# Second attention: the attended values leave their bank on VectorE, behind the routing steps, and no longer on ScalarE

## The reference

```python
# second attention (H = 8 heads of DH = 128; context and tokens are its keys and values)
xn = _layernorm(x, gamma_media, beta_media); ln = _layernorm(latents, gamma_lat, beta_lat)
q = ln @ Wq + bq
k, v = split(concatenate([xn, ln], axis=1) @ Wkv + bkv)
sim  = einsum('bhid,bhjd->bhij', q * DH ** (-0.5), k)
attn = softmax(sim, axis=-1)
out  = einsum('bhij,bhjd->bhid', attn, v) ... @ Wo + bo
x = x + tanh(g_xattn[1]) * out
# second expert layer: the two best of 8 experts for each token
logits = xf @ router_w.T; top_w, top_i = lax.top_k(softmax(logits), 2)
...
x = x + tanh(g_ffn[1]) * sum over the two of share * w_down(silu(w_gate x) * (w_up x))
```

## Time and profile before

| what | value |
| --- | --- |
| median of 3 timed runs | 1478.63 us (1478.35 to 1478.68) |
| profiled execution, first to last instruction | 1498.2 us |
| PE busy | 1377.6 us, 92% of the span |
| DVE busy | 953.4 us, 64% |
| ACT busy | 1012.3 us, 68% |
| POOL busy | 523.2 us, 35% |
| copy of the attended values (L2051, ACT) | 64 times, 616 ns in the middle |

### The profile page before, as it was taken

How to read it: one execution, slowest core, us unless ns; L and a number is a source line. 1 busy time by engine, 2 the same in 40 slices (tenths; PEclk the granted TensorE clock), 3 DMA queues, 4 the chain that set the end, 5 groups by cost and what they waited for, 6 DMA issues and landing times. The chain is left out here.

```text
span 1498.2 us, 33716 instructions
## 1 busy us (share of the span) xinstructions
PE 1377.6 (92%) x12029; PEld 1171.5 (78%) x12029; DVE 953.4 (64%) x2374; ACT 1012.3 (68%) x2019; POOL 523.2 (35%) x510
## 2 busy tenths in 40 slices
PE   5898699899999999999999999988999999876985
PEld 4887588788888888888888888877778888755773
DVE  6998767666766767667667666552455555654455
ACT  5887487577677676776776767647788888633552
POOL 3112355322322322323223223302235555635553
PEclk9999899999999999999999999999999999998998
DMA  8300100399940000000000000022000000022236
GB/s 221 88 1 1 58 2 1 77 176 102 102 30 2 2 1 2 2 2 2 2 2 1 2 1 2 1 73 57 1 29 14 17 16 16 30 69 63 76 97 174
DMA packets 124980, 60.46 MB, mean 40 GB/s; under 512 B 41945, under 2 KB 120241, under 8 KB 124690
## 3 DMA queue, kind: packets, MB, share of 16 engines
q1 hardware_dynamic: 120274, 48.92, 18.2%
q0 software_dynamic: 4544, 9.38, 1.9%
HBM read 28.84 MB, written 29.44 MB: 39 GB/s over the span
## 5 line engine op out<-in xcount | busy, mean ns | idle before, releaser
L1349 DVE SCALAR_TENSOR_TENSOR hidden<-psU,b_cols,gelu 128x512 f32<-128x512 f32 x256 | 191.4, 750 | 170.1 <-ACT gelu L1474 104.9
L1474 ACT ACTIVATE gelu<-psG,b_cols 128x512 f32<-128x512 f32 x256 | 176.2, 689 | 109.6 <-PE psG L142 96.2
L1296 POOL TENSOR_TENSOR combine_sum<-combine_sum,combineT 128x512 f32<-128x512 f32 x48 | 63.3, 1319 | 294.9 <-ACT combineT L1488 294.9
L1325 POOL TENSOR_TENSOR dispatchT<-dispatchT,dispatch_inv 128x512 f32<-128x512 f32 x64 | 67.7, 1057 | 232.6 <-DVE dispatch_inv L1453 232.6
L1608 PE MATMUL psU<-w_down,hidden 128*64 128x128 f32 x2048 | 123.4, 273 | 0.0
L1608 PE MATMUL psDown<-w_down,hidden 128*64 128x128 f32 x2048 | 122.7, 273 | 0.0
L1861 POOL TENSOR_TENSOR probs<-probs,row_sum 128x512 f32<-128x512 f32 x64 | 66.2, 1035 | 143.6 <-DVE row_sum L1974 142.6
L1608 PEld LDWEIGHTS psU<-w_down,hidden 128*64 128x64 f32 x2048 | 113.2, 137 | 1.3 <-issue 1.2
L1608 PEld LDWEIGHTS psDown<-w_down,hidden 128*64 128x64 f32 x2048 | 113.9, 137 | 0.1
L140 PE MATMUL psG<-slots_hi,w_gate_hi 128*128 128x512 f32 x256 | 105.9, 414 | 1.1 <-ACT gelu L1474 0.6
L2038 ACT ACTIVATE probs<-psS,neg_max 128x128 f32<-128x128 f32 x256 | 91.2, 384 | 22.8 <-DVE neg_max L1971 18.4
(11 more groups left out here) (406 smaller groups left out, 3617.6 us busy)
## 6 DMA issues: line engine op xcount, KB each, us to landing
sorted_x<-empty_rows SPq DMA_DIRECT2D x1, 12736.0 KB, 77.5
tile_rows<-sorted_x SPq DMA_DIRECT2D x78, 65.0 KB
sorted_x<-empty_rows SPq DMA_DIRECT2D x1, 4544.0 KB, 29.9
expert_ys<-expert_y SPq DMA_DIRECT2D x16, 256.0 KB, 3.7
x<-in_x SPq DMA_DIRECT2D x8, 256.0 KB, 5.9
ctx<-in_ctx SPq DMA_DIRECT2D x8, 256.0 KB, 5.9
w_gate_raw<-in_L_ffn_Wg SPq DMA_DIRECT2D x1, 2048.0 KB, 10.9
w_up_raw<-in_L_ffn_Wu SPq DMA_DIRECT2D x1, 2048.0 KB, 16.1
```

What stands on the lines that cost most here:

```text
L1325: pool.tensor_tensor(e[:], e[:], over(rb[:], SEQ, 2), ALU.mult).then_inc(s["eb_normed"], 1)
L1349: dve.scalar_tensor_tensor(hid[e][:, half, :], U[half][:], bcol[:, 1, 4 * ch + 2 * e + half:][:, 0:1], gel[half][:], ALU.add, ALU.mult).th ...
L1474: act.activation(gel[half][:], G[half][:], ACT.Gelu, bias=bcol[:, 0, 4 * ch + 2 * e + half:][:, 0:1]).then_inc(s["gelu"], 1)
```

## The change

The copy from `Y` to `yT` moves from ScalarE to VectorE. On ScalarE it stood behind the copy of the turned probabilities (and a query eviction) of the same slot and ahead of the input evictions and of ScalarE's routing steps. On VectorE it stands at the end of the slot, behind `route(o, j)`. Its two waits move with it: for the value product (`av`), and for the output product that last read this half of the buffer (`out`). The engine operation becomes a tensor copy, with the same source and destination. Nothing else is changed; lines behind the insertion move by seven.

```diff
@@ VectorE, slot()
                 route(o, j)
+                if exists(o, j, 3):
+
+                    m = (j - 3) % OB
+                    need(dve, s["av"], n - 2)
+                    need(dve, s["out"], 4 * o + (j - 3) // 2 - 1)
+                    dve.tensor_copy(yT[(m // 2) % 2][:, :, (m % 2) * SEQ:(m % 2 + 1) * SEQ],
+                                    Y[:].rearrange("p (h n) -> p h n", h=H)).then_inc(s["yT"], 1)
@@ ScalarE, slot()
                 if 2 <= j <= 5 and has_head(o):
                     q_out(o, par, 2 * (j - 2) + 1)
-                if exists(o, j, 3):
-
-                    m = (j - 3) % OB
-                    need(act, s["av"], n - 2)
-                    need(act, s["out"], 4 * o + (j - 3) // 2 - 1)
-                    act.copy(yT[(m // 2) % 2][:, :, (m % 2) * SEQ:(m % 2 + 1) * SEQ],
-                             Y[:].rearrange("p (h n) -> p h n", h=H)).then_inc(s["yT"], 1)
```

## The result

| | before | after |
| --- | --- | --- |
| median of 5 runs, same chip | 1478.35 us (1476.96 to 1478.68) | 1489.08 us (1487.72 to 1490.11) |
| ratio, 95% interval | 1 | 1.007 (1.006 to 1.0081) |

The account below looks back on a forecast made before the run. TensorE was taken to set the pace, held up partly by ScalarE's copy. Early gains of -2.03 us and +6.72 us in octet 7 and the tail gave +4.7, so 1483.3 us, range 1478.5 to 1487.5.

Parts of the forecast that it names:

- the price of a copy: Each copy on VectorE, PSUM to SBUF: 0.69 us, with bounds of 0.19 and 0.69 + 0.38 us.
- the gain in octets 0 and 1: Output product's waits for the copy shrink: -0.85 us in slot 0.7, -0.59 in 1.1, -0.84 in 1.7.
- the five slots o.7: Slot 7 of octets 2 to 6: copy starts behind destination steps, wait stays, +0.12 us each, +0.60 together.
- the predicted waits of over 2.5 us in 7.3 and of about 4 in 7.5: Octet 7, slots 3 and 5: output product waits for VectorE's late copy; its start shifts +1.50 and +4.23 us.
- wait of some 6 us ahead of the last value products: End of the stage, behind slot 8.1: expected TensorE wait of some 6 us; value product shifted +6.62 us.
- they depend on a query product and its own eviction, not on this copy; freeing ScalarE does nothing for them: TensorE's waits for evicted queries (qAT) were claimed not to depend on the copy; no gain counted.
- the 0.3 that I allowed: Steady octets 3 to 6: the forecast counts as wrong if they change by more than 0.3 us each.
- Rival 3: Last output product: new idle time lowers TensorE's clock, another +2.4 us, total +7.1, 1485.8 us; 16%.
- My sum for the late copies: Octet 7 and tail: copies queued behind routing delay output products, reaching +6.72 us at the last one.
- The relief wins: All 13 waits for the copy go, gaining 11.5 us, 1467.1 us; 8% together with a milder form.
- A wash: Octet 7: routing shortens and the copy costs 0.19 us, leaving +0.7 us, 1479.3 us; 14%.
- The stage's tail: Milder rival: tail hidden since experts wait for their first tile; only -2.0 us left, 1476.6; 8% with full relief.

Follow-up runs that it names:

- e6: The changed kernel with the copies of slots 1 and 2 in octets 2 to 6 back on ScalarE: 1485.87 us, ratio 1.0054.
- e4: The changed kernel plus 2, 4 and 3 unread matmuls where TensorE waits in slots 7.3, 7.5 and 8.2: 1484.95 us, ratio 1.0036.
- e3: The changed kernel with all 64 copies on VectorE ahead of the slot's routing steps instead of behind them: 1478.45 us, ratio 0.9995.
- e7: The kernel before, with VectorE copying ahead of routing only in slots 0 and 6 of each octet and 7.2: 1473.02 us, ratio 0.9949.
- e2: The kernel before, with the copy on VectorE behind routing only from octet 7 on: 1489.46 us, ratio 1.007.
- e8: The kernel before, with VectorE copying behind routing only in slots 0 and 6 of each octet and 7.2: 1476.58 us, ratio 0.9981.
- e5: The kernel before, with ScalarE's copy made to wait for VectorE's routing steps from octet 7 on: 1489.48 us, ratio 1.0071.
- e9: The changed kernel with the three copies of slots 7.2, 7.4 and 8.1 back on ScalarE: 1481.33 us, ratio 1.0017.

## Why the prediction was wrong

**Right: the price of a copy.** I took 0.69 us from an eviction of the same size. The copy's line in after, ns shortest/median/longest:

```profile
L1990 DVE COPY yT<-psY x64: 658/690/692, 1038.4 to 1324.5; 128x512 f32<-128x512 f32 x64
```

Neither the gaps in the destination nor GpSimd's passes made it longer, so both ends of my range for it were too far out.

**Right: the gain in octets 0 and 1, and the five slots o.7 nearly.** -2.36 at slot 1.7 against -2.28. The +0.12 that I had priced for each o.7, 0.60 in all, came to nothing.

**Right: where the late copies are, and the first one's size.** The product of 7.3 is 1.53 us late, against 1.50; the predicted waits of over 2.5 us in 7.3 and of about 4 in 7.5 are 2.46 and 3.80 on the weight loads. The "wait of some 6 us ahead of the last value products" was a slip: my own sum has 6.62 - 4.78 of new wait there beside the old 0.77, 2.6 us, and it measured 2.70. The copy of 7.2 is late because of what stands ahead of it, as said (VectorE's timeline):

```profile
1286.99 0.69 DVE L1990 COPY yT<-psY 128x512 f32<-128x512 f32 x1
1287.59 0.68 DVE L1971 TENSOR_REDUCE neg_max<-psS 128x4 f32<-128x512 f32 x1
```

**Wrong: "they depend on a query product and its own eviction, not on this copy; freeing ScalarE does nothing for them".** That holds for freeing ScalarE, but loading VectorE reaches the evicted queries by another way, and I named the test that it fails: octets 3 to 5 change by 0.56 each, over the 0.3 that I allowed. It goes like this. By the traces' own clocks TensorE's scores of slot 3.1 start 1.80 us earlier in after (1130.42 against 1132.22). But neg_max of slot 3.0 stands behind the eight normalising passes, which stand behind a copy, and starts only 0.53 earlier (1129.33 against 1129.86). GpSimd's two passes of slot 3.1 follow it, 0.54 earlier than before (timeline of POOL):

```profile
1133.64 1.05 POOL L1861 TENSOR_TENSOR probs<-probs,row_sum 128x512 f32<-128x512 f32 x1
1134.64 1.27 POOL L1869 TENSOR_TENSOR latents_lo<-kv_inT,latents_hi 128x512 fp32r<-128x512 f32 x1
```

The top step on VectorE, 1.88 earlier, has moved with TensorE and now meets both of them with its first operation of two SBUF inputs. VectorE in after:

```profile
1134.10 1.87 DVE L442 TENSOR_TENSOR is_max<-logits,top 128x32 f32<-128x32 f32 x1
...
1136.90 0.69 DVE L1990 COPY yT<-psY 128x512 f32<-128x512 f32 x1
1137.51 0.68 DVE L1971 TENSOR_REDUCE neg_max<-psS 128x4 f32<-128x512 f32 x1
```

and the same instruction before, which met only the end of the second pass:

```profile
1135.98 0.52 DVE L442 TENSOR_TENSOR is_max<-logits,top 128x32 f32<-128x32 f32 x1
```

The scores of slot 3.2 ended at 1136.32; neg_max starts 1.2 us later. ScalarE's exponentials wait for it, behind them in its queue stands the next query eviction, and TensorE waits for that (one row of ScalarE, one of TensorE):

```profile
1138.22 0.37 ACT L2045 ACTIVATE probs<-psS,neg_max 128x128 f32<-128x128 f32 x1 [0.48 <-DVE neg_max L1971]
```

```profile
1140.94 0.47 PE L140 MATMUL psQ<-latents_hi,A_hi 128*128 128x512 f32 x1 [0.37 <-ACT qAT L2033]
```

From the query product of the slot before to this one it is 3.05 us where it was 2.46 without a wait: 0.6 us in each of octets 3 to 6. e6 takes the copy from between top step and neg_max and gets them back although L442 still takes 1.88 there. Octet 2 of after is the other half of the evidence: there the copy stands behind the top step of 2.1 as well, but the top step starts in a gap between GpSimd's two passes and is held by one of them alone, in its second operation,

```profile
1097.66 0.19 DVE L442 TENSOR_TENSOR is_max<-logits,top 128x32 f32<-128x32 f32 x1
1097.89 1.17 DVE L444 TENSOR_TENSOR is_max<-is_max,order 128x32 f32<-128x32 f32 x1
```

so neg_max of 2.2 starts 0.5 us behind its scores and not 1.2, the next query product follows after 2.46 us as before, and the octet takes 36.44 us against 36.47. So it takes both: the copy, and the top step ahead of it held by both passes. In octets 3 to 6 this cost 2.4 us that my sum had at nothing; the missing 0.60 of the slots o.7 and smaller ones take part of it back, which leaves 1.56 us of my error (-0.47 against -2.03).

The Trainium skill ("SBUF — State Buffer", "Who interferes with whom") states that a VectorE instruction with two SBUF inputs contends with a GpSimd instruction that reads SBUF, while one with at most one SBUF input, outside the modes that use both ports, doesn't. The trace agrees on both: L442 was held for 1.87 us under two passes, and the copy, which has no SBUF input, never took over 0.692 us, though nine of the 64 ran beside a GpSimd tensor operation.

**Wrong: the clock, which the forecast had at nothing.** Rival 3 named the mechanism, with 2.4 us at the last output product alone and 16%. It fell in three places, and e4 prices it at 4.7 us. My sum for the late copies without it was good: with the clock held, e4's shifts from the product of 7.1 on, in the order of the table, are 1.54, 4.28, 3.82, 4.92, 6.76, 6.90 and 6.91 us, against my 1.50, 4.23, 3.79, 4.78, 6.62, 6.72 and 6.72. The argument against it, that the stretch stayed at 1.00 with 7 us idle, was the faulty one: they were mostly single waits of 0.2 to 1.5 us (seven, 5.8 us in all), spread over the stretch, and my own steps predicted single waits of 2.5 and 4 us. I had the two lengths side by side without drawing the conclusion. Nor would one row have settled it: the trace of before does have a wait of 2.23 us with the clock at 1.00 behind it (1028.21, shown with e3), and the same wait ended at 0.52 in e3. It was a risk at three places, to be priced at all three.

The error is then 11.10 - 4.69 = 6.41 us from the first neg_max on: 1.56 in the steady octets and 4.85 behind slot 7.1, where the clock's 4.7 is nearly all of it. The shorter prologue of after takes 0.39 off, which I can't claim either way.

**The rivals.** The relief wins: wrong for this change, though e7 shows that it is there at another place. A wash: octets 0 to 6 were one, but by gains and losses that cancel; the tail was not, and the copy took 0.69 us, not the 0.19 of that rival. The stage's tail was not hidden behind the expert stage: the first expert transposes moved by all of it.

## What to carry to other kernels

Moving work from a busy engine to a less busy one is a question of its place in the new queue, not of the engine: the same copy cost 10.7 us behind the routing, nothing ahead of it, and gained 6.8 us when it moved in the right slots only. Look for the longest stretch in which the new engine works without a gap between the moment when the data are ready and the new place, and carry the delay on to what stands behind it, one engine further than feels needed. Where the sum predicts single TensorE waits well beyond those that the stretch has now (here 2.5 and 4 us against 1.5), give the sum a second value with the instructions behind each such wait at the low clock, and compare kernels by their timed medians, since one profile can fall on either side.

## What the runs showed of the hardware

- In after TensorE's granted clock fell to mixes of 0.62 to 0.81 within a stage that was otherwise busy, behind single waits of 2.3 to 3.6 us, and the sixteen matmuls behind them took up to 3.65 us in place of 2.05.
- The same wait in the same code does not always have that effect. Behind 2.2 us in slot 0.2 the clock was low in two of twelve profiles. Behind the 2.27 us of 7.3 the product took 3.62 us in after and 2.05 in e2 and e6, and in e8 behind 2.41; behind 1.96 us in e5 it took 2.05, behind 1.68 in e9 3.64. Behind 3.6 us it was slow in all four. What decides is open.
- Matmuls with no use, in TensorE's idle time ahead of a late operand, held the clock at 1.00 and were worth 4.7 us of the stage (5.0 timed); three of them where waits were short were worth nothing.
- A VectorE operation on 32 columns that takes 0.19 us alone took 0.52, 1.07, 1.17 or 1.87 us, by how much of GpSimd's one or two passes it met.
